# Second attention: value bias folded away, both normalisations on another engine, another order

## The reference

```python
x = _layernorm(x + _L0_ffn_ref(...))          # its result: "incoming rows"
c_k = x @ w_dk + b_dk;  k = c_k @ w_uk + b_uk
c_v = x @ w_dv + b_dv;  v = c_v @ w_uv + b_uv
q, k = rope(x), rope(k)                       # 16 heads of 8 features
attn = softmax(q @ k.T / sqrt(8))             # 256 x 256 for each head
out = (attn @ v) @ w_o + b_o
x = _layernorm(x + out)                       # second normalisation; its rows are routed to experts
```

## Time and profile before

| what | us |
|---|---|
| median of three runs | 1338.38 |
| profiled execution | 1332.43 |
| its span in the trace | 1330.7 |
| TensorE busy in the span | 1246.4 |
| VectorE busy | 971.2 |
| ScalarE busy | 862.8 |
| GpSimd busy | 624.0 |
| first exps to last exps of this attention | 775.2 to 1144.5 |

### The profile page before, as it was taken

The page is one execution under the profiler, slowest core; times in us unless marked ns, Lnnn a source line. Parts: engine busy times, 40 slices in busy tenths (PEclk is TensorE's granted clock), DMA queues, the critical chain, the costliest instruction groups (busy, mean ns, idle before and its releaser), DMA issues. The chain is left out here.

```text
span 1330.7 us, 33931 instructions
## 1 busy us (share of the span) xinstructions
PE 1246.4 (94%) x10925; PEld 1033.7 (78%) x10925; DVE 971.2 (73%) x2849; ACT 862.8 (65%) x2233; POOL 624.0 (47%) x965
## 2 busy tenths in 40 slices
PE   5999999999999999999999789999999999869996
PEld 4888888888888888899999666666666665558985
DVE  6787887778888888786776658888888886353443
ACT  4777777777777776656655356666666664758863
POOL 2244444444444444463553534555565542336773
PEclk9999999999999999999999979999999997989998
DMA  8012121121212121023224032202215001013326
GB/s 278 22 38 85 49 72 57 64 67 53 75 46 83 38 89 54 14 74 116 66 59 134 33 117 83 82 22 91 81 39 196 15 11 72 33 36 110 107 74 198
DMA packets 56451, 100.88 MB, mean 76 GB/s; under 512 B 11056, under 2 KB 46256, under 8 KB 53616
## 3 DMA queue, kind: packets, MB, share of 16 engines
q1 hardware_dynamic: 46704, 80.06, 19.4%
q0 software_dynamic: 9088, 18.89, 4.0%
q10 hardware_dynamic: 576, 0.86, 0.2%
HBM read 78.81 MB, written 62.06 MB: 106 GB/s over the span
## 5 line engine op out<-in xcount | busy, mean ns | idle before, releaser
L628 ACT ACTIVATE a_prob<-psum,a_nmx 128x128 f32<-128x128 f32 (+1 forms) x512 | 208.6, 425 | 74.2 <-DVE a_nmx L991 74.2
L861 POOL TENSOR_TENSOR a_prob<-a_prob,a_rl 128x128 f32<-128x128 f32 (+1 forms) x256 | 124.7, 510 | 242.7 <-DVE a_rl L995 242.1
L2681 DVE TENSOR_REDUCE f_nmx<-psum 128x4 f32<-128x1024 f32 x120 | 146.7, 1222 | 33.8 <-PE psum L214 33.4
L2432 ACT ACTIVATE a_prob<-psum 128x1024 f32<-128x1024 f32 x128 | 130.3, 1021 | 37.3 <-PE psum L2158 37.2
L635 ACT ACTIVATE a_probt<-psum 128x768 f32<-128x768 f32 x128 | 105.0, 820 | 75.9 <-PE psum L1438 75.9
L908 POOL DMA_INDIRECT yt<-a_yrow,a_dest x78 | 81.0, 1038 | 94.0 <-ACT a_yrow L677 76.0
L628 ACT ACTIVATION_READ_ACCUMULATOR a_prob<-psum,a_nmx 128x1 f32 x512 | 107.5, 210 | 0.0
L1438 PE MATMUL psum<-ident,a_prob 128*128 128x128 f32 x768 | 105.3, 273 | 1.1 <-DVE a_prob L1001 0.7
L980 DVE TENSOR_TENSOR a_qkt<-psum,a_bqk 128x512 f32<-128x512 f32 x128 | 88.4, 691 | 19.5 <-PE psum L109 16.8
L107 PE MATMUL psum<-a_x_h,a_wqk_h 128*128 128x256 f32 x312 | 93.3, 299 | 2.7 <-DVE a_wqk_l L1178 2.6
L1795 POOL DMA_INDIRECT yt<-m_yrow,m_dest x78 | 75.6, 969 | 41.0 <-issue 21.7
(11 more groups left out here) (413 smaller groups left out, 3811.0 us busy)
## 6 DMA issues: line engine op xcount, KB each, us to landing
xs<-in_fill SPq DMA_DIRECT2D x144, 264.0 KB, 4.2
a_xrow<-xs SPq DMA_DIRECT2D x39, 132.0 KB, 2.1
m_xrow<-xs SPq DMA_DIRECT2D x39, 132.0 KB, 2.3
f_yin<-yt SPq DMA_DIRECT2D x18, 256.0 KB, 2.8
w<-in_w SPq DMA_DIRECT2D x16, 256.0 KB, 3.4
f_yin<-yt SPq DMA_DIRECT2D x7, 512.0 KB, 7.7
f_w<-in_wr SPq DMA_DIRECT2D x2, 1284.0 KB, 6.9
xs<-in_fill_idle SPq DMA_DIRECT2D x2, 1056.0 KB, 6.8
```

Source lines behind the costliest of these rows:

```text
L628: last = nc.scalar.activation(prob[:, hp % 4, h, at], S[:, 2 * (hp % 2) + h, at], ACT.Exp, bias=nmx[:, hp % 4, q, h:h + 1], accum_out=lsum ...
L861: last = nc.gpsimd.tensor_tensor(prob[:, hp % 4, 0, at], prob[:, hp % 4, 0, at], rl[:, hp % 4, 0, q:q + 1].to_broadcast(prob[:, hp % 4, 0, ...
L2432: nc.scalar.activation(prob[:, k % 2, 2 * (t % 2):2 * (t % 2) + 2, :], ST[:, 2 * (t % 2):2 * (t % 2) + 2, :], ACT.Exp, scale=SCALE).then_i ...
L2681: nc.vector.reduce_max(f.nmx[:, :, 2 * i:2 * i + 2].rearrange("p q h -> p h q"), R.rearrange("p h (q k) -> p h q k", q=QB), AX.X, negate=T ...
```

## The change

- `values` moves from VectorE to ScalarE and becomes a plain copy. A one-column matmul before the loop forms b_uv times w_o in `ST[:, 3, 0:1]`, ScalarE adds b_o to it (`bout`), and `tail_residual` uses bout. b_uv is loaded as one column instead of spread.
- `incoming_rows` and `normalise` move to ScalarE: `Identity` with scale = the inverse deviation and bias = a shift, -mean times the inverse deviation, which VectorE computes (`incoming_shift`, `rows_shift`).
- `add_rows` on GpSimd is split: `weighed_rows` (f_ysum) stays, `add_rows` (f_res) goes behind `running_counts`, `keep_rows` and `name_rows`; running_counts goes ahead of keep_rows.
- The order changes on TensorE (router to the start, turn behind scores(1), outputs(0) ahead of tail_columns, tail_project behind scores(3), tail_rows behind scores(4), tail_store behind scores(5), incoming behind outputs(2), ranks ahead of latents), on ScalarE (router first, high and tail_store later, the new calls between) and on VectorE (incoming_variances ahead of maximum(1), rotate_k behind it, variances ahead of route_rows).

The calls in the end part, behind the batches, keep VectorE's `normalise(1, B + 1)`.

```diff
@@ -270,12 +270,14 @@
+    def weighed_rows(m):
+        pool.wait_ge(f.yw_done, m + 1)
+        nc.gpsimd.tensor_tensor(f.ysum[:], f.yw[:, :, 0, :], f.yw[:, :, 1, :], ALU.add).then_inc(f.sum_done, 1)
+
     def add_rows(m):
-        pool.wait_ge(f.yw_done, m + 1)
+        pool.wait_ge(f.sum_done, m + 1)
         if not isinstance(m, int) or m > 0:
             pool.wait_ge(f.rows_done, m)
-        nc.gpsimd.tensor_tensor(f.ysum[:], f.yw[:, :, 0, :], f.yw[:, :, 1, :], ALU.add).then_inc(f.sum_done, 1)
-        pool.wait_ge(f.sum_done, m + 1)
         nc.gpsimd.tensor_tensor(f.res[:], f.ysum[:], g.x1[:, bass.ds(m * T, T)].rearrange("p (q n) -> p q n", q=QB), ALU.add
@@ -285,9 +287,10 @@
         weigh(m, p, turn)
+        weighed_rows(m)
         add_rows(m)
-    return rotate_x, rotate_k, weigh_rows, weigh, add_rows, incoming_power
+    return rotate_x, rotate_k, weigh_rows, weigh, weighed_rows, add_rows, incoming_power
@@ -2111,7 +2116,7 @@
             rows_of(3, 1)
-            for dst, src in ((buv[:], d["b_uv"].partition_broadcast(P)), (rw32[:], d["r1w"]), (rb[:], d["m1_rb"]),
+            for dst, src in ((buv[:], d["b_uv"].unsqueeze(1)), (rw32[:], d["r1w"]), (rb[:], d["m1_rb"]),
                              (before32[:], d["before"]), (b1[:], d["m1_sb1"]), (sb2[:], d["m1_sb2"])):
@@ -2224,6 +2229,8 @@
             values(0)
+            pe.wait_ge(loaded, LOADS * 16)
+            nc.tensor.matmul(ST[:, 3, 0:1], wu[:, 2, :], buv[:], start=True, stop=True).then_inc(bout_ps, 1)
             pe.wait_ge(rx_done, 3)
@@ -2256,9 +2263,14 @@
                         part_of_scores(t, 1, p).then_inc(st_ps, 1)
+                    if routed:
+                        pe.wait_ge(nt_done, n)
+                        pe.wait_ge(osb_done, n * NGR + 1)
                     if tail:
                         pe.wait_ge(exp_done, n * NPR - 1)
                         maxima(n + 1, MT)
+                    if routed:
+                        router(columns_of(n - 2), PV)
                     if second:
                         if tail:
@@ -2270,9 +2282,6 @@
                     scores(0)
                     pair(0)
-                    if routed:
-                        pe.wait_ge(nt_done, n)
-                        pe.wait_ge(osb_done, n * NGR + 1)
                     if turned:
                         pe.wait_ge(k_done, n + 3)
@@ -2282,36 +2291,36 @@
                             pe.wait_ge(v_done, 1)
                         values(1 - p)
-                    if routed:
-                        router(columns_of(n - 2), PV)
+                    if tail:
+                        pe.wait_ge(o_done, n + 1)
+                    else:
+                        pe.wait_ge(bout_done, 1)
+                    scores(1)
                     if turned:
                         turn()
-                    if tail:
-                        pe.wait_ge(o_done, n + 1)
-                    scores(1)
                     pair(1)
+                    scores(2)
+                    if routed:
+                        pe.wait_ge(lg_done, n - 1)
+                    pe.wait_ge(v_done, n + 1)
+                    outputs(0, p, n)
                     if second:
                         pe.wait_ge(v_done, n + 2)
...
                     if tail:
                         tail_columns(n + 1, MISC)
-                    scores(2)
+                    pair(2)
+                    scores(3)
                     if tail:
                         tail_project(columns_of(n - 1), n + 1)
-                    pair(2)
+                    pair(3)
+                    scores(4)
                     if routed:
-                        pe.wait_ge(lg_done, n - 1)
-                    pe.wait_ge(v_done, n + 1)
-                    outputs(0, p, n)
-                    scores(3)
-                    pair(3)
+                        pe.wait_ge(osb_done, n * NGR + 2)
                     if tail:
                         pe.wait_ge(rt_done, n + 1)
                         tail_rows(n + 1)
-                    if routed:
-                        pe.wait_ge(osb_done, n * NGR + 2)
-                    scores(4)
                     if routed:
                         router_rows(n - 1, PV)
@@ -2323,24 +2332,25 @@
                     outputs(1, p, n)
                     pair(4)
+                    scores(5)
                     if tail:
                         tail_store(1 - p, n + 1)
-                    scores(5)
                     scores(6)
                     pair(5)
+                    outputs(2, p, n)
                     if fresh:
                         if tail:
                             pe.wait_ge(nt_done, n + 1)
                         incoming(n + 4)
-                    outputs(2, p, n)
+                    if routed:
+                        pe.wait_ge(osb_done, n * NGR + 4)
                     pair(6)
                     scores(7)
+                    if routed:
+                        ranks(n - 1, PV)
                     if fresh:
                         pe.wait_ge(rx_done, n + 4)
                         latents(columns_of(n + 3), n + 4)
-                    if routed:
-                        pe.wait_ge(osb_done, n * NGR + 4)
-                        ranks(n - 1, PV)
                     pair(7)
                     if routed:
@@ -2436,13 +2446,33 @@
+            def values(p, n):
+
+                act.wait_ge(v_ps, n)
+                nc.scalar.activation(v[:, p, :, :, 0:DH1], MISC[:, 0:BT].rearrange("p (q h e) -> p q h e", q=QB, h=H1), ACT.Copy
+                                     ).then_inc(v_done, 1)
+
+            def incoming_rows(n):
+                act.wait_ge(cshift_done, n)
+                for q in range(QB):
+                    last = nc.scalar.activation(f.rows[:, q, :], f.res[:, q, :], ACT.Identity, scale=f.crstd[:, q:q + 1],
+                                                bias=f.cshift[:, q:q + 1])
+                last.then_inc(f.rows_done, 1)
+
+            def normalise(p, n):
+                act.wait_ge(shift_done, n)
+                for q in range(QB):
+                    last = nc.scalar.activation(nrm[:, p, q, 0:P], MISC[:, q * P:(q + 1) * P], ACT.Identity, scale=rstd[:, q:q + 1],
+                                                bias=shift[:, q:q + 1])
+                last.then_inc(nrm_done, 1)
+
             def tail_columns(n, bank):
...
                 act.wait_ge(y_ps, n)
-                nc.scalar.activation(rt[:], MISC[:, 0:T], ACT.Identity, bias=bias[:, 3:4]).then_inc(rt_done, 1)
+                nc.scalar.activation(rt[:], MISC[:, 0:T], ACT.Identity, bias=bout[:]).then_inc(rt_done, 1)
@@ -2466,6 +2496,11 @@
             two_stacks(0, 1, ST[:, 0:2, :], 1)
+            act.wait_ge(v_set, 1)
+            values(0, 1)
+            act.wait_ge(bout_ps, 1)
+            nc.scalar.activation(bout[:], ST[:, 3, 0:1], ACT.Identity, bias=bias[:, 3:4]).then_inc(bout_done, 1)
+            act.wait_ge(bout_done, 1)
             latents(0, 3, PV)
@@ -2474,39 +2509,48 @@
                     second, turned, fresh = within(n + 1), within(n + 2), within(n + 3)
                     tail = follows(n)
+                    if routed:
+                        router(n - 1, PV)
                     if second:
                         two_stacks(NGR // 2, 1 - p, R, n * 2 + 2)
+                    exps(0, n)
+                    exps(1, n)
+                    if turned:
+                        act.wait_ge(ksin_done, n + 3)
+                    if second:
+                        values(1 - p, n + 2)
+                    exps(2, n)
                     if turned:
                         high(0, rq, q_total, q_high, n + 1)
-                    exps(0, n)
-                    if routed:
-                        router(n - 1, PV)
-                    exps(1, n)
                     if tail:
                         tail_columns(n + 1, MISC)
+                    outputs(0, n)
+                    exps(3, n)
                     if turned:
                         high(1, rk, k_total, k_high, n + 1)
-                    exps(2, n)
                     if tail:
                         tail_residual(n + 1)
-                    outputs(0, n)
-                    exps(3, n)
                     exps(4, n)
                     if turned:
                         two_stacks(0, p, R, n * 2 + 3)
+                    if tail:
+                        normalise(1 - p, n + 1)
                     outputs(1, n)
+                    exps(5, n)
                     if tail:
                         tail_store(columns_of(n - 1), n + 1)
-                    exps(5, n)
+                    if fresh:
+                        incoming_rows(n + 4)
+                    outputs(2, n)
                     if fresh:
                         incoming(columns_of(n + 3), n + 4)
                     exps(6, n)
-                    outputs(2, n)
                     exps(7, n)
                     if fresh:
                         latents(1 - p, n + 4)
```

(50 more changed lines are left out.)

10 lines of the change are left out of this document (6 added, 4 removed).

## The result

The changed kernel took 1373.06 us (median of four, 1361.05 to 1385.48); the kernel before, run beside it on the same chip, 1336.5 us (1330.26 to 1340.44). The ratio is 1.025, 95% interval 1.017 to 1.033: slower by 2.5%. The forecast of 1332 us and its range to 1344 are both wrong. The profiled execution is the slowest of the four (1385.48 us, span 1383.7, clock 0.944; the one before: 1332.43, span 1330.7, clock 0.981), so the difference of the two traces, 53.0 us, overstates that of the medians, 36.6.

What follows compares the result with a forecast made beforehand. It took TensorE and VectorE stepping through pairs, maximum after maximum, as the bound, at most 2.5 us a batch to gain. Batches -6.0 and +2.1, start +1.0, total -2.9: 1329.5 or 1335.5, middle 1332 us; range 1317 to 1344.

Steps and rivals of the forecast that it cites:

- the sum of a batch: Second attention, three stretches of one batch added: 11.6 + 7.03 + 4.65 = 23.3 us, even and odd alike.
- first piece: Start of batch to two_stacks(0): 11.6 us for both kinds, before 11.57 in odd and 13.11 in even batches.
- f_rk meets at most their last tenths: VectorE's f_rk, now later, barely overlaps GpSimd's four scatters and f_yw; 1.5 us go in even batches of the loop.
- the variances (0.9) ahead in the room that a_v and f_rk left: VectorE ahead of maximum(1): the 0.9 us of variances fit in freed room, so pair(2) still waits 0.15 us.
- Piece two: From two_stacks(0) to pair(6): 7.03 us against 6.63 before, dearer by 0.4, as maximum(5) waits behind f_xtl.
- Piece three: From pair(6) to the next batch's start: 4.65 us against 4.75, ranks ahead of latents taking its wait away.
- f_rk's 1.5: Time f_rk loses to GpSimd's f_yw in even batches; its removal was in batches 4, 6, 8, 10 gaining 1.3 each.
- The start: Before the loop, TensorE waits for loads ahead of latents and ScalarE gets extra work: 0.8 to 1.4 us late, 1.0 taken.
- The clock adds some to it: Remark on the range: another start may place the first batches' 17 us at 1.2 GHz differently; no size given.
- Relief comes through: Rival: VectorE's lighter batch shortens TensorE's waits; 12.5 us off with half gone, 28 with all; middle 1322; chance 0.28.
- Shifts starve: Rival: VectorE's shifts lose to GpSimd's running_counts, late by 1.35 us; fourteen batches lose 1.25 each; +14.6, 1353; chance 0.12.
- The collision only moves: Rival: f_rk comes 0.2 us earlier, falls under f_yw again, even batches keep their 1.5 us; +3, 1340; chance 0.10.

Runs made afterwards that it cites:

- old_piece_one: Changed kernel with turn back ahead of scores(1) on TensorE, and rotate_k ahead of and incoming_variances behind maximum(1) on VectorE; 1356.97 us, ratio 1.004.
- after_variances_back: Changed kernel with only VectorE's steps put back, rotate_k ahead of maximum(1) and incoming_variances behind it; turn stays behind scores(1); 1376.90 us, ratio 1.028.
- after_turn_back: Changed kernel with only turn put back ahead of scores(1) on TensorE; incoming_variances stay ahead of maximum(1); 1373.30 us, ratio 1.018.
- rk_first: Kernel before with one swap on VectorE, rotate_k (f_rk) ahead of values (a_v); 1346.71 us, ratio 1.004.
- moves_old_order: Kernel before with values, incoming_rows and normalise moved to ScalarE, all else in the old order; 1367.74 us, ratio 1.018.
- order_on_vector: Changed kernel's order with values, incoming rows and normalise all back on VectorE; 1358.80 us, ratio 1.013.
- norms_only: Kernel before with only the two normalisations on ScalarE, values left on VectorE, old order; 1352.63 us, ratio 1.009.
- before_no_filler: Kernel before without stir, the six matmuls a batch whose result is overwritten; 1350.75 us, ratio 1.007.
- start_without_wait: Changed kernel with the output bias's one-column matmul and its activation behind latents and keys, so TensorE does not wait for loads first; 1372.38 us, ratio 1.024.
- after_start_filled: Changed kernel with the output bias's matmul behind keys and five stir matmuls in the start of its stage; 1361.28 us, ratio 1.015.

## Why the prediction was wrong

**The step that failed is the sum of a batch, in its first piece:** "I take 11.6 for both kinds". It measured 12.55 in odd and 12.76 in even batches. Inside it, two sentences. "f_rk meets at most their last tenths" was right for f_rk (0.43 to 0.64), but the lock was looked for at the operation that had shown it, not at those that take its place under f_yw: f_cveps took 0.57 to 0.78 instead of 0.17 in even and 0.33 in odd batches. And "the variances (0.9) ahead in the room that a_v and f_rk left": there was no room, since turn behind scores(1) made VectorE idle 0.42 us ahead of f_ksin; maximum(1) came 1.3 us later in odd batches, and pair(2) waited 0.59 (odd) to 0.78 (even) where 0.15 was reckoned. turn's move stood in the change and was given no price. old_piece_one, with exactly these steps back, has the predicted 11.6. after_variances_back and after_turn_back show that both steps are needed.

**The other pieces held.** Piece two: 7.03 forecast, 7.15 measured. Piece three: 4.65 and 4.84. a_nrm 0.81 us for two, as worked out; each shift 0.15 behind the gap, with no late start. f_xtl of tail_store is 5.44 us behind two_stacks(0) (5.8 forecast), with VectorE idle ahead of it for f_xth, and VectorE is at 19.0 to 19.2 us a batch (18.5), ScalarE at 17.1 (17). One smaller slip is in the sum: it charges batches 1, 12 and 13 with 0.2 us each, where its own 23.3 us against 23.04, 22.89 and 22.47 make 0.3, 0.4 and 0.8.

**The gain was not there either.** Even batches were to win 1.3 us by f_rk's 1.5. rk_first takes those 1.5 off VectorE and gets 0.65 in even batches, 0.25 net over a pair. moves_old_order takes them off too and its even batches stay at 24.5. Of the 1.7 us between an even and an odd batch 0.6 aren't f_rk's; the forecast had taken nearly equal numbers (1.5 and 1.70) for cause and effect.

**The start** was reckoned at 1.0 us late. It is 9.5, with 27.3 us more at 1.2 GHz, and with the matmul moved behind keys 3.3, with 6.8 more. The clock explains nearly all of both; the waits themselves cost no more than was reckoned.

**The clock had no term in the sum.** The prediction wrote "The clock adds some to it" and gave it no number. It is near half of the loss between the medians, 16 us, and two thirds or more between the profiled runs, 35 to 41 of 53. The earlier trace rows had the warning, 17 us at 1.2 GHz around the start and a kernel that carries `stir` matmuls whose results are thrown away. before_no_filler shows what they are worth.

**The rivals.** None was the case. "Relief comes through" is refuted by order_on_vector in the new order, the same batches with VectorE at 20 us and at 19, and by norms_only in the old one, longer batches with 0.8 us less. "Shifts starve": shifts 0.15, refuted; its time, 1353, was on the right side for the wrong reason. "The collision only moves" named the mechanism but held it to f_rk and to even batches, at 6 us; it moved to another operation, and to all batches.

By the Trainium skill ("SBUF — State Buffer", section SBUF: two separate sides) whoever starts first has the port pair. The rows do not bear that out for starts as recorded: f_rk in the earlier trace rows and in after_variances_back, and f_cveps in after_turn_back, start 0.01 to 0.56 us ahead of f_yw and end behind it. It would have made no difference to the sum.

What stays open is which waits make the granted clock fall. The same waits stand in batches 5 to 12 of the changed kernel, at 1.00 throughout, and in batches 1 to 4, where it falls; in start_without_wait and after_start_filled it falls in batches 9 and 10 as well. The Trainium skill ("TensorE: Matmul & The Clock Gate", Part 1) has the gate follow how busy the array has lately been; that fillers raise the clock and their removal lowers it agrees (0.976 against 0.954; 0.943 against 0.971). How the 16 us of clock between the medians divide over the stage isn't known. Between the two profiled executions, of 104.9 more us at 1.2 GHz 27.3 lie ahead of batch 1, 41.0 in batches 1 to 13, 14.0 in batch 14 and 22.6 behind it, where the code is nearly all the same. It is open, too, whether that last part is the change's or chance: in the profiled executions of the experiments the same stretch took 203.3 to 212.9 us, and that of the kernel before, at 202.8, is the shortest of all.

## What to carry to other kernels

Before a reordering, write down for each operation of VectorE what GpSimd will be doing at that time, for the new neighbours too: a collision that goes away at one operation can turn up at the next, and a 128x2 operation is held up too (0.17 us alone, 1.10 in after_turn_back). Follow each moved step to the first thing that waits for it, here turn to f_ksin to maximum(1), before calling room free. Judge a moved operation by the queue that it moves into, not by that engine's idle time: a_v behind exps(1) made TensorE wait 1.15 us. Where a kernel carries filler matmuls or shows a clock below 1.00 anywhere, give the clock a term: here each us at 1.2 GHz costs 0.34 us, and the change cost as much again in clock as in waits.

## What the runs showed of the hardware

- A VectorE operation that met GpSimd's f_yw ended just after it, at both sizes seen: f_cveps (128x2) at 1031.93 for f_yw's 1031.90, and at 977.91 for 977.87; f_rk (128x256), at 978.93 and 1003.94, some 0.3 us after f_yw (978.64 and 1003.65).
- The time at 1.2 GHz explains nearly all that the 77 runs of the unchanged kernel differ by (0.336 us for each us, correlation 0.99), so a single run is read with its clock: of the first four runs of the change, from 1361.05 to 1385.48 us, clocks were 0.967 to 0.944.
- Removing work can slow the kernel: without stir the loop's batches at full clock are 21.8 and 23.7 instead of 22.9 and 24.6 us, and the kernel takes 10 us more.
